# Attention scores of all eight head pairs by one full-precision product instead of three reduced ones

## The reference

```python
def reference(x, W_Q, b_Q, W_K, b_K, W_V, b_V, W_O, b_O, weight, gate_w, lora_U, lora_V):
    # attention, on layernorm(x)
    Q = einsum('btd,hkd->bthk', xn, W_Q) + b_Q      # K and V alike
    scores = einsum('bqhk,bshk->bhqs', Q, K) / sqrt(64)
    attn = softmax(scores)
    y = einsum('bqhk,hdk->bqd', einsum('bhqs,bshk->bqhk', attn, V), W_O) + b_O
    x = x + layernorm(y)
    # feed-forward, on layernorm(x): a base product and 8 gated low-rank ones
    gate = softmax(xt @ gate_w.T)
    z = xt @ weight.T + einsum(gate, lora_V, einsum(xt, lora_U)) / 16
    return x + layernorm(z)
```

## Time and profile before

| | |
|---|---|
| median of three runs | 979.77 us (979.45 to 981.7) |
| the profiled execution | 980.0 us, of which the span on the engines is 978.2 us |
| granted TensorE clock, mean | 0.993 of full |
| TensorE busy | 960.1 us, 98% of the span |
| VectorE / ScalarE / GpSimd busy | 909.9 / 887.7 / 759.9 us |

### The profile page before, as it was taken

How to read it: one execution, slowest core, us unless ns; L and a number is a source line. 1 busy time by engine, 2 the same in 40 slices (tenths; PEclk the granted TensorE clock), 3 DMA queues, 4 the chain that set the end, 5 groups by cost and what they waited for, 6 DMA issues and landing times.

```text
span 978.2 us, 28088 instructions
## 1 busy us (share of the span) xinstructions
PE 960.1 (98%) x8582; PEld 773.8 (79%) x8582; DVE 909.9 (93%) x1666; ACT 887.7 (91%) x3183; POOL 759.9 (78%) x746
## 2 busy tenths in 40 slices
PE   8999999999999999999999999999999999999995
PEld 7777888778888878888877888877888887888874
DVE  6999999999999999999999999999999999999972
ACT  4999999999999999999999999999999999999872
POOL 2777988888888788878878878887888878877862
PEclk9999999999999999999999999999999999999997
DMA  7276775666676666676666676666677666667560
GB/s 267 53 164 139 172 163 135 142 151 138 157 172 140 138 151 138 145 177 146 138 152 138 139 172 159 137 145 146 138 161 169 139 137 153 138 149 173 136 145 11
DMA packets 58467, 143.32 MB, mean 147 GB/s; under 512 B 16960, under 2 KB 25664, under 8 KB 58432
## 3 DMA queue, kind: packets, MB, share of 16 engines
q1 hardware_dynamic: 58432, 142.89, 63.2%
HBM read 6.50 MB, written 4.19 MB: 11 GB/s over the span
## 4 chain that ended last, share of the span: by engine, by line
PE 93%; DVE 2%; SPq 2%; ACT 1%; issue 1%; DMA 0%; POOL 0%; POOLq 0%; DVEq 0%; ACTq 0%
PE o_ps L487 24%; PE st_ps L462 21%; PE extra_ps L521 9%; PE qk_ps L428 6%; PE qk_ps L429 6%; PE qk_ps L430 6%; PE xv_ps L442 4%; PE extra_ps L358 3%; PE xv_ps L444 3%; PE xv_ps L443 3%; PE extra_ps L543 2%; SPq L313 2%; PE extra_ps L556 2%; PE extra_ps L558 1%; PE xv_ps L358 1%
## 5 line engine op out<-in xcount | busy, mean ns | idle before, releaser
L1795 POOL TENSOR_TENSOR probs<-probs,inv_sum 128x1024 f32<-128x1024 f32 x256 | 484.4, 1896 | 115.2 <-DVE inv_sum L1315 108.0
L850 ACT ACTIVATE probs<-st_ps,neg_max 128x256 f32<-128x256 f32 x1024 | 476.9, 496 | 33.7 <-DVE neg_max L1307 31.8
L1307 DVE TENSOR_REDUCE neg_max<-st_ps 128x4 f32<-128x1024 f32 x256 | 308.6, 1206 | 11.3 <-PE st_ps L462 10.5
L1326 DVE STREAM_TRANSPOSE probs_b<-probs 128x1024 f32<-128x1024 f32 x252 | 309.2, 1230 | 1.1 <-POOL probs L1795 1.1
L487 PE MATMUL o_ps<-probs_t,v_sb 128*64 128x256 f32 x2048 | 249.3, 385 | 1.2 <-DVE o_lo L1341 0.7
L850 ACT ACTIVATION_READ_ACCUMULATOR probs<-st_ps,neg_max 128x1 f32 x1024 | 231.5, 226 | 0.0
L487 PEld LDWEIGHTS o_ps<-probs_t,v_sb 128*64 128x64 f32 x2048 | 135.8, 136 | 80.8 <-DVE o_lo L1341 10.4
L462 PE MATMUL st_ps<-qk_hi 64*128 64x256 f32 x1024 | 162.7, 314 | 1.6 <-ACT probs L850 0.9
L836 ACT CAST qk_hi<-qk_ps 128x512 fp32r<-128x512 f32 x256 | 153.2, 599 | 11.1 <-PE qk_ps L430 6.2
L462 PE MATMUL st_ps<-qk_lo,qk_hi 64*128 64x256 f32 x1024 | 145.3, 279 | 0.0
L462 PE MATMUL st_ps<-qk_hi,qk_lo 64*128 64x256 f32 x1024 | 144.8, 278 | 0.0
(11 more groups left out here) (140 smaller groups left out, 1946.7 us busy)
## 6 DMA issues: line engine op xcount, KB each, us to landing
probs_t<-probs_b SPq DMA_DIRECT2D x1008, 128.0 KB, 2.4
out<-x_all SPq DMA_DIRECT2D x31, 128.0 KB, 1.9
x_all<-in_x SPq DMA_DIRECT2D x1, 3840.0 KB, 17.9
probs_b<-in_w_v SPq DMA_DIRECT2D x1, 512.0 KB, 4.2
probs_b<-in_w_o SPq DMA_DIRECT2D x1, 512.0 KB, 6.6
probs_b<-in_w_q SPq DMA_DIRECT2D x1, 384.0 KB, 5.0
probs_b<-in_w_k SPq DMA_DIRECT2D x1, 384.0 KB, 5.8
x_all<-in_x SPq DMA_DIRECT2D x2, 128.0 KB, 3.1
```

Source lines behind the costliest of these rows:

```text
L850: last = nc.scalar.activation(probs[n][:, h, j, :], st_ps[p % 2][:, (2 * h + j) * T:(2 * h + j + 1) * T], ACT.Exp, bias=neg_max[n][:, h, j ...
L1307: nc.vector.tensor_reduce(neg_max[p % N_PROBS][:, :, :].rearrange("p h j -> p (h j)"), st_ps[p % 2][:, :].rearrange("p (j s) -> p j s", j= ...
L1326: nc.vector.transpose(probs_b[chunk % 2][:, :, :, 2 * NT * n:2 * NT * (n + 1), :].rearrange("p i t n q -> p n t i q"), probs[p % N_PROBS][ ...
L1795: nc.gpsimd.tensor_tensor(probs[n][:, :, :, :].rearrange("p h j s -> p (h j) s"), probs[n][:, :, :, :].rearrange("p h j s -> p (h j) s"), ...
```

## The change

All eight pairs are put into a new list `WHOLE`. For these `qk_hi` is no longer rounded: ScalarE's copy writes fp32. `scores` makes one plain fp32 product of queries and keys for each half of the queries and each head, in place of the three of fp32r: 4 calls of 256 columns for a pair, where there were 12. The remainders `qk_lo` are gone from VectorE and GpSimd, and the copies `qk_full` from ScalarE. A projection waits for ScalarE's copy alone (`lo_written`). The orders of all engines are written anew.

```diff
-POOL_LO = (1, 5,)
-VECTOR_LO = tuple(p for p in range(PAIRS) if p not in POOL_LO)
+POOL_LO = ()
+WHOLE = (0, 1, 2, 3, 4, 5, 6, 7,)
+VECTOR_LO = tuple(p for p in range(PAIRS) if p not in POOL_LO + WHOLE)
...
             if p in POOL_LO:
                 return qk_pool_lo_ready, len(POOL_LO) * b + POOL_LO.index(p) + 1
+            if p in WHOLE:
+                return qk_hi_ready, PAIRS * b + p + 1
             return qk_lo_ready, len(VECTOR_LO) * b + VECTOR_LO.index(p) + 1
...
                 terms = ((q_hi, k_hi), (q_hi, k_lo), (q_lo, k_hi))
+                if p in WHOLE:
+                    terms = ((q_hi.bitcast(F32), k_hi.bitcast(F32)),)
                 for j in range(NT):
                     for t, (q, k) in enumerate(terms):
                         for h in range(2):
                             last = nc.tensor.matmul(st_ps[p % 2][:, (2 * h + j) * T:(2 * h + j + 1) * T],
                                                     tile(q, j)[head_rows(h), :], k[head_rows(h), :],
-                                                    start=(t == 0), stop=(t == 2))
+                                                    start=(t == 0), stop=(t == len(terms) - 1))
...
             def qk_hi(b, p):
                 act.wait_ge(qk_projected, PAIRS * b + p + 1)
-                nc.scalar.copy(qk_hi_sb[p % N_QK][:, :], qk_ps[:, :]).then_inc(qk_hi_ready, 1)
+                dst = qk_hi_sb[p % N_QK][:, :]
+                nc.scalar.copy(dst.bitcast(F32) if p in WHOLE else dst, qk_ps[:, :]).then_inc(qk_hi_ready, 1)
...
             def body(i, r):
                 transpose_xn(i, free=(v_copied[3], i))
-                transpose_y(i - 3, free=(yt_ready, i - 2))
-                project_qk(i - 1, 6, 1 - r)
-                scores(i - 1, 5)
+                project_qk(i - 1, 7, 1 - r)
                 probs_v(i - 2, 2, r)
                 probs_v(i - 2, 3, r)
```

More of the change, by code:

```diff
@@ L765, in _ @@
             probs_v(30, 1, 0)
[L766 to L768 removed]
+            transpose_y(29, free=(yt_ready, 30))
+            scores(31, 3)
             scores(31, 4)
@@ L962, in _ @@
-            copy_v(1, 0, 1)
+            exponentials(0, 5, 1)
+            exponentials(0, 5, 0)
             qk_hi(1, 0)
[L964 to L968, removed]
             exponentials(0, 6, 0)
             exponentials(0, 6, 1)
-            qk_hi(1, 2)
-            copy_v(1, 2, 1)
+            copy_v(1, 0, 1)
+            qk_hi(1, 1)
             exponentials(0, 7, 1)
             exponentials(0, 7, 0)
+            copy_v(1, 1, 1)
@@ L975, in _ @@
+            qk_hi(1, 2)
+            exponentials(1, 0, 1)
+            exponentials(1, 0, 0)
             qk_hi(1, 3)
+            copy_v(1, 2, 1)
+            exponentials(1, 1, 0)
+            exponentials(1, 1, 1)
             copy_v(1, 3, 1)
-            exponentials(1, 0, 0)
-            exponentials(1, 0, 1)
             qk_hi(1, 4)
-            exponentials(1, 1, 1)
-            exponentials(1, 1, 0)
-            qk_full(1, 5)
+            exponentials(1, 2, 0)
             qk_hi(1, 5)
-            xt_high(2, 0)
@@ L1031, in _ @@
             qk_hi(2, 7)
+            copy_x1t(0)
+            exponentials(2, 4, 1)
             attention_hi(1, 1)
-            copy_v(3, 0, 1)
+            qk_hi(3, 0)
             exponentials(2, 5, 0)
             exponentials(2, 5, 1)
-            qk_hi(3, 0)
+            qk_hi(3, 1)
+            exponentials(2, 6, 0)
+            qk_hi(3, 2)
             exponentials(2, 6, 1)
             gate_exponentials(0)
+            exponentials(2, 7, 1)
+            exponentials(2, 7, 0)
+            copy_v(3, 0, 1)
@@ L1052, in _ @@
-            copy_v(3, 2, 1)
-            attention_hi(1, 3)
-            copy_z(0)
-            exponentials(3, 1, 0)
             qk_hi(3, 4)
             exponentials(3, 1, 1)
+            attention_hi(1, 3)
+            exponentials(3, 1, 0)
+            exponentials(3, 2, 1)
+            exponentials(3, 2, 0)
+            copy_v(3, 2, 1)
+            qk_hi(3, 5)
+            square_z(0)
+            copy_z(0)
+            qk_hi(3, 6)
+            exponentials(3, 3, 0)
+            exponentials(3, 3, 1)
@@ L1107, in body @@
-                qk_hi(i, 5)
+                exponentials(i, 1, 0)
+                exponentials(i, 1, 1)
+                square_z(i - 3)
+                qk_hi(i, 3)
+                copy_v(i, 1, r)
+                copy_z(i - 3)
+                attention_hi(i - 2, 3)
+                exponentials(i, 2, 1)
+                exponentials(i, 2, 0)
+                qk_hi(i, 4)
                 exponentials(i, 3, 1)
                 exponentials(i, 3, 0)
+                qk_hi(i, 5)
+                copy_yt(i - 2)
@@ L1110, in body @@
+                copy_v(i, 2, r)
+                exponentials(i, 4, 0)
+                exponentials(i, 4, 1)
+                qk_hi(i, 6)
+                copy_v(i, 3, r)
                 attention_hi(i - 1, 0)
                 square_y(i - 2)
-                qk_hi(i, 6)
-                exponentials(i, 4, 1)
-                exponentials(i, 4, 0)
+                exponentials(i, 5, 1)
+                exponentials(i, 5, 0)
             body(4, 0)
@@ L1165, in _ @@
-            attention_hi(30, 2)
-            copy_ut(29)
+            gate_exponentials(29)
+            qk_hi(31, 7)
+            copy_v(31, 2, 1)
+            exponentials(31, 5, 1)
+            copy_ut(29)
+            attention_hi(30, 2)
+            square_z(29)
+            copy_v(31, 3, 1)
             exponentials(31, 5, 0)
-            square_z(29)
+            copy_z(29)
+            attention_hi(30, 3)
             exponentials(31, 6, 1)
-            attention_hi(30, 3)
-            copy_z(29)
@@ L1596, in body @@
-                transpose_blocks(i - 2, 7)
-                row_max(i - 1, 2)
-                qk_lo(i - 1, 4)
-                invert_sum(i - 1, 1)
-            run(dve, 5, B - 1, body)
-            spread_x(31)
+                invert_sum(i - 2, 4)
+            body(6, 0)
+            run(dve, 7, B - 1, body)
+            attention_lo(27, 0)
+            row_max(28, 6)
+            residual_x1(26)
+            xt_low(29, 1)
+            spread_x1(26)
+            spread_landed(LN_X1, 26)
+            transpose_blocks(28, 3)
@@ new lines, in _ @@
+            aggregate_x1(26)
+            invert_sum(28, 5)
+            row_max(28, 7)
+            gate_max(26)
+            scale_gate_max(26)
+            attention_lo(27, 1)
+            invert_sum(28, 6)
+            transpose_blocks(28, 4)
+            apply_gate(26)
+            row_max(29, 0)
+            attention_lo(27, 2)
+            invert_sum(28, 7)
+            transpose_blocks(28, 5)
+            row_max(29, 1)
+            transpose_blocks(28, 6)
+            spread_x(31)
+            invert_sum(29, 0)
@@ new lines, in _ @@
+            row_max(29, 2)
+            invert_sum(29, 1)
+            attention_lo(27, 3)
+            transpose_blocks(28, 7)
+            row_max(29, 3)
+            invert_sum(29, 2)
+            transpose_blocks(29, 0)
+            transpose_blocks(29, 1)
+            row_max(29, 4)
+            invert_sum(29, 3)
+            transpose_blocks(29, 2)
+            row_max(29, 5)
+            invert_sum(29, 4)
+            transpose_blocks(29, 3)
+            attention_lo(28, 0)
+            row_max(29, 6)
```

808 lines of the change are left out of this document (358 added, 450 removed).

## The result

| | before | after |
|---|---|---|
| median | 979.61 us | 1017.38 us |
| ratio | | 1.0373, 95% interval 1.0359 to 1.0387 |
| profiled execution, span | 978.2 us | 1015.7 us |
| loop body: start of the transposes of xn, from sequence 5 to sequence 30 (counted from 0), divided by 25 | 29.07 us | 30.36 us |

The change makes the kernel 3.7% slower. 1014 us was forecast, with a range of 1002 to 1030.

A forecast was written before the change was run, and what follows sets the result against it. TensorE's own stream was taken as the bound: 980.0 us plus 34.1 us (39.4 from longer streams, −6.8 from entries, the rest rounding) gave 1014.1, with the median 0.2 us lower, so 1014 us; range 1002 to 1030.

The forecast's parts named there:

- The bound: Whole kernel: TensorE's own work sets the time; work taken from other engines gives nothing directly.
- What was taken away: VectorE, GpSimd and ScalarE lose 130.4, 82.2 and 37.9 us, coming to 780, 678 and 850 us busy.
- The stream: Scores: a pair takes four steps of 0.217 us, 0.868 against 0.714 us; longer streams add 39.4 us.
- The entry: Going into a run of scores: 0.14 us against 0.20, with more runs, −6.8 us in all; at most 0.20 us.
- The start: First 55 us: remainders on the chain hold 2.6 us; gain taken as 0, 2.6 us the largest.
- The new wait: Loop body, run of pairs 4 and 5: pair 5's copy comes 0.3 to 0.4 us late, 1025 us; chance 0.10.
- Without overlap: Scores: row halves go one at a time, eight steps a pair, 222 us more, 1236 us; chance 0.04.
- weight loads in the open: Scores: each step grows by 0.11 us because loads wait for products to leave, 1127 us; chance 0.02.
- Faster steps: Scores: an fp32 record carries both passes at once, a step of 0.11 us, 902 us; chance 0.04.

The follow-up runs named there:

- The second experiment: The kernel before, its order and three fp32r products kept, all hi times hi, with remainders and full copies struck: 976.59 us, ratio 0.9967.

## Why the prediction was right

**The bound.** Right. TensorE's own stream set the time before and after. The second experiment shows the counterpart: over 200 us of work taken from the other engines gave 3.2 us.

**What was taken away.** GpSimd's and ScalarE's busy times came near their forecasts (676 for 678, 860 for 850). VectorE's is 805 and not 780. I subtracted the remainders' whole time, but busy time counts overlapping instructions once, and neighbours of a remainder had overlapped it. It made no difference, as VectorE doesn't bound.

**The stream.** Right to the record: eight records for a pair, two at a time, 0.216 us a step where 0.217 was taken from the values' products. That column halves in fp32 and row halves in fp32r together tell what row halves in fp32 do held; the price of the opposite is measured at 1238 us for the forecast 1236.

**The entry.** This term was mis-sized. I took 0.14 us, from `probs_v`, and the dearer bound of 0.20 us was right: 1.06 − 4 × 0.216 = 0.196 us. All scores after come to 63 × 1.93 + 130 × 1.06 = 259.4 us instead of 249.7, 9.7 us more. The reason I gave for the lower value, that long steps leave room for the next weight load, seems to look at the wrong load. The first step is longer than the later ones by 0.10 us here and by 0.05 us in `probs_v`; the loads take 187 ns and 137 ns. The difference of the first steps is the difference of the loads, which points to the first product's own load as the one that nothing covers. Whole-array work of the kernel before shows the same two sizes. The first product of `xv_ps` behind `probs_v`, with a load of 187 ns, takes 0.43 us, and 0.23 behind other whole-array work, 0.20 more. Two transposes, with loads of 142 ns, take 0.37 us and not 0.22, 0.15 more. From the chain of waits and from the records by line:

```profile
502.01 0.43 PE xv_ps L442
506.32 0.23 PE xv_ps L442
L442 PEld LDWEIGHTS xv_ps<-wv_hi,xt_hi x128: 186/187/286, 13.4 to 931.1; 128*128 128x128 f32 x128
L358 PEld LDWEIGHTS xv_ps<-ident,xn x64: 137/142/143, 9.3 to 899.1; 128*128 128x128 f32 x64
```

This is read from the starts; no experiment changed a load.

**The start.** I took 0 and kept 2.6 us of gain as a bound; without the remainders the old order gained 3.2 us, 2.7 of them there. How much of this the new order keeps isn't shown by a run.

**What is left.** By the runs' own lengths the scores cost 259.4 − 215.6 = 43.8 us, and the spans differ by 37.5. About 3 of the 6.3 us between lie in the bodies. Less its scores and its four runs of `probs_v`, a body of before is 29.07 − 6.70 − 4 × 1.88 = 14.85 us of whole-array work, and one of after 30.36 − 8.10 − 7.52 = 14.74 us: 0.11 × 27 = 3 us. I had put this at nothing, since the number of whole-array stretches doesn't change. A third of it is there without the remainders in the old order too (29.03 us a body); the rest came with the new order, and why is open. The other 3 us lie in the start and the end, and I haven't placed them. The late copy of pair 5 has no part in this, as it shows in neither of these two kernels.

**Luck in the number.** The entries cost 9.7 us more than forecast, and the 6 us just named go the other way. That 1014 us came within 4 us of 1017.38 is partly because these errors cancel. What the forecast had right by its reason are the longer streams: 39.4 us forecast, and 38.5 us measured for the product alone in the order of before.

**The rivals.** The new wait didn't come in the changed kernel; it stood there with fp32r at 0.05 us a body, so the margin was real but small. Without overlap, and weight loads in the open: out, since the steps are 0.216 us. With all products on one half they still are (3.65 us for 16), and there each next load can only go to the half that is at work. The rule of the Trainium skill ("TensorE: Matmul & The Clock Gate", "The mechanism") that a load overlaps matmuls in flight only on another row group does not describe these products. Faster steps: out. By the four passes of the Trainium skill ("FP8 and Floating Point Precision", "TensorE Precision Notes") my estimate had been 1035 us; the trace puts a call at 2 × 0.216 us against 0.118 for fp32r, 3.7 times and not 4, and that is the difference that matters at three calls against one.

## What to carry to other kernels

Before giving one engine more work to relieve others, find who sets the time stretch by stretch; here over 200 us of work taken from three engines at 78 to 93% gave 3 us, and 0.15 us more for each of 256 pairs on the fourth cost 38. Price a form that no row shows from the two rows that share one trait each with it, and take its going-in cost, as the starts here suggest, from the one that shares its weight load, not its step. Check the work that the change leaves alone too: its length moved by 3 us with the order. In an order written by hand a call also covers waits of others: moving the scores of one pair by a few places cost 20 to 46 us, where one or two entries of 0.20 us a body were to be saved.

## What the hardware showed that I had not expected

TensorE doesn't need neighbours in the order to fill both row halves. With two calls of head 0 ahead of head 1's, two records still start together, at 0.10 us more for a run of two pairs; a strict order would have cost about 167 us or more, and records on one half do go one by one (1238 us).

The first weight load of a run seems to show in its length: 0.10 us where loads take 187 ns, 0.05 us where they take 137, on top of the 0.09 us by which the first start comes late after another kind of work (0.196 less 0.10 us for `scores`, 0.14 less 0.05 for `probs_v`). This is read from the starts alone.
